# A fused block of three attentions, a feed-forward, experts and a mixture of depths: one output product and two batches of comparisons put in another order

## The chip, the cores and the metric

The kernel runs on one core of a Trainium2 chip. The metric is the device time of one execution in microseconds (us). The engines of a core run their own instruction queues: TensorE (PE) multiplies matrices and transposes, VectorE (DVE) reduces, adds and splits numbers, ScalarE (ACT) does exponents, Gelus and copies, GpSimd (POOL) does normalizations, powers and indirect transfers, and SyncE (SP) issues DMAs. They meet through semaphores: an instruction that waits holds up everything behind it in its queue.

## The reference

Eight batches of 256 tokens with 256 features go through four residual steps. Only the last two touch the change.

```
x = x + attention_block(layernorm(x), ctx)      # cross, self, feed-forward
x = x + experts(layernorm(x))                   # top 2 of 8, capacity
x = x + mha(layernorm(x), ctx, ctx)             # 16 heads: here "third attention"
x = x + mod(layernorm(x))

def mod(h):                                     # mixture of depths
    scores = einsum('bsd,d->bs', h, w_router)
    top_scores, top_idx = top_k(scores, 128)    # half the tokens of a batch
    selected = take(h, top_idx)
    processed = gelu(selected @ W1 + b1) @ W2 + b2
    return h.at[top_idx].add(sigmoid(top_scores) * processed)
```

## The kernel before

An attention works in items: item n is one batch of one attention, and items 16 to 23 are batches 0 to 7 of the third one. For an item TensorE makes scores for eight pairs of heads twice: once for the row maxima that VectorE reduces (L785), once transposed for ScalarE's Exp (L807, into T_PS). Behind two Exps each a group of probability products (L853) fills half of a bank, ScalarE copies it to oext (L1164), and behind the fourth such copy TensorE transposes oext (L827). VectorE divides by the sums, TensorE transposes back (L249), ScalarE and VectorE write aT_hi and aT_lo, the upper and lower half of each number, and TensorE makes the output product with three matmuls for each tile (mm3, L216 to L218: high times high, low times high, high times low). VectorE adds its result to xres (L1645, semaphore res_s). The transposes of the next item's oext wait for that res_s.

The mixture of depths works in pairs of batches: pair j is batches 2j and 2j+1. mod_select(j) turns scores into a one-hot selection. GpSimd spreads a batch's scores, TensorE transposes them (L982), and VectorE counts for each token how many scores stand above it (L1818 and L1819, twice each), adds (trank, L1820), and compares with the slot numbers (oh, L1824). I call these eight instructions a batch's comparisons. TensorE then gathers with that one-hot (L996), transposes it (L1001), and mod(j) does the first product (mm3 with hT and m_lo), ScalarE's Gelus (L1258) and copies (L1268), VectorE's lower halves (L1841), the second product for each batch (mm3 with kst and qst), VectorE's result in three instructions (L1850 to L1852: proc, its upper and lower half), TensorE's scatter product with the transposed one-hot (L1055 and L1056), and VectorE's addition to xres (L1859, x4 for a pair).

No scheduler decides the order on an engine. Every part is a generator that yields the time at which its next step is due, and side_by_side runs the step with the least due time, on each engine apart. The tables PE_ORDER, ACT_ORDER, POOL_ORDER and DVE_ORDER override this: an entry "A": "B" puts step A straight behind step B, and behind(...) chains a list of them. "attention 22.23" is step 23 of item 22 on that engine. On TensorE the steps of an item from 9 on are: Exp scores 9, 10, 11, products 12, scores 13, 14, products 15, scores 16, 17, 18, products 19 and 20, the transposes of oext 21, those of the divided output 22, the output product 23. "mod 0.0" to "mod 0.3" are four quarters of the first half of pair 0's first product, six matmuls each. On VectorE "mod_select j.1" is the comparisons of the second batch of pair j, and "mod j.5" the result of that pair's second batch.

On ScalarE the four Gelus of pair 0's first half wait for the last of these four quarters, and the order there is: copy of item 23's third product group, first Gelu, copy of the fourth group, the other Gelus. The first Gelu needs a table load of its own.

Of the kernel before, what the change touches and what calls it, by code (L numbers as in the profile page):

```python
# [94 lines left out]
def behind(*steps):  # L95

    return dict(zip(steps[1:], steps))


def build(nc, x, ctxT, mask, wA, colA, rowA, fi, fo, fib, rw, rb, ein, eout, wC, colC, rowC, colV, w1, w2, b1, out):  # L100
# [21 lines left out]
    with scope[0] as root:  # L122
# [312 lines left out]
        def mod_bank(i):  # L435
# [24 lines left out]
            **behind("mod_select 0.2", "attention 23.14", "attention 23.15", "mod_select 1.0", "attention 22.22", "attention 23.16", "mod 0.0", "mod 0.1", "attention 23.17",  # L460
                     "mod 0.2", "mod 0.3", "attention 23.18", "attention 23.19", "attention 23.20", "attention 22.23", "attention 23.21", "mod 0.4", "mod 0.5",
                     "attention 23.22", "mod 0.6", "mod 0.7", "attention 23.23", "mod_select 1.1", "mod_select 1.2", "mod 0.8", "mod_select 2.0"),
        }
        ACT_ORDER = {
# [33 lines left out]
            **behind("mod_select 0.1", "attention 21.10", "attention 21.11", "attention 20.13", "attention 21.12", "attention 22.8", "mod_select 0.2", "attention 22.9",  # L498
                     "mod_select 1.0", "mod_select 1.1", "attention 21.13", "attention 22.10", "attention 23.8", "attention 22.11", "attention 22.12", "mod 0.0", "mod 0.1",
                     "attention 23.9", "attention 23.10", "mod 0.2", "mod 0.3", "mod_select 1.2", "attention 23.11", "attention 23.12"),  # L500
        }

        with nc.Block() as block:
# [1411 lines left out]
```

How the kernel before makes its waits and increments, by code:

```python
    def __call__(self, ins):  # L64
        self.n += 1
        ins.then_inc(self.sem, 1)
        self.eng.wait_ge(self.sem, self.n)
# [439 lines left out]
                def setup():  # L507
# [16 lines left out]
                    sp.dma_start(rows[:, 2:8, :], rowA[2:8].unsqueeze(0).to_broadcast([P, 6, D])).then_inc(sm["small_ld"], 16)  # L524
                    sp.dma_start(fibc[:], fib).then_inc(sm["small_ld"], 16)
                    sp.dma_start(rbr[:], rb.to_broadcast([P, 8])).then_inc(sm["small_ld"], 16)
                    sp.dma_start(rw_raw[:], rw.rearrange("(k p) n -> p k n", p=P)).then_inc(sm["small_ld"], 16)
                    sp.dma_start(b1c[:], b1).then_inc(sm["small_ld"], 16)
                    sp.wait_ge(sm["ident_s"], 3)
                    for i in range(NE * CAP // P):
                        yield 28 + 4 * i
                        sp.dma_start(moe_in[i * P:(i + 1) * P, :], zeros[:]).then_inc(sm["zero_out"], 16)
                    sp.dma_start(moe_out[NE * CAP:NE * CAP + 1, :], zeros[0:1, :]).then_inc(sm["zero_out"], 16)
                    yield STEP * B + 32
                    sp.wait_ge(sm["h_ready"], B)
                    sp.dma_start(rows[:, R_CO:R_CBE + 1, :], rowA[R_FO:R_FBE + 1].unsqueeze(0).to_broadcast([P, 3, D])).then_inc(sm["rowsF_ld"], 16)
                    yield T_F0 + 8
                    sp.wait_ge(sm["h_ready"], NA)
# [537 lines left out]
                def mask_rows():  # L1076
                    yield -93
                    act.wait_ge(sm["mask_s"], 1)
                    for c in range(2):
```

## Time and profile before

| | |
|---|---|
| median of 3 runs | 857.49 us (852.05 to 859.93) |
| the profiled execution's own time | 855.1 us |
| its span | 853.1 us |
| TensorE busy, share of the span | 729.4 us, 85% |
| VectorE | 648.7 us, 76% |
| ScalarE | 455.6 us, 53% |
| GpSimd | 409.2 us, 48% |
| mean granted TensorE clock | 0.929 |

The span runs from the first to the last instruction on the core; the execution's own time has some 2 us around it. A row of a timeline gives the start, the duration, engine, line, operation, output and inputs, and in brackets how long the engine had been idle and what released it. Neighbouring equal instructions are merged into one row. A matmul's duration covers its whole way through the array, so matmuls in a group start closer together than they last.

### The profile page before, as it was taken

Reading aid. Unit: us, or ns where it says so; the run is one execution under the profiler, and the core shown is the slowest. Engines: PE = TensorE matmul, PEld = TensorE weight load, DVE = VectorE, ACT = ScalarE, POOL = GpSimd, SP = SyncE. Lnnn points to the kernel's source line nnn. Section 1 sums busy time; section 2 is a strip of 40 time slices with the busy share of each in tenths; the row PEclk is TensorE's granted clock in tenths of the full one; section 3 lists DMA queues with packets and bytes.
Section 4 is the critical chain, followed back from the end, with each engine's and each line's share of the span. In section 5 each row is a group of like instructions: output and inputs, shape, how many; then the busy total and the mean of one; then the engine's idle time right before and its main releaser. Section 6 shows DMA issues by size and latency. Waiting matters only on the chain.

```text
span 853.1 us, 18296 instructions
## 1 busy us (share of the span) xinstructions
PE 729.4 (85%) x7218; PEld 607.8 (71%) x7218; DVE 648.7 (76%) x1250; ACT 455.6 (53%) x695; POOL 409.2 (48%) x395
## 2 busy tenths in 40 slices
PE   5788999999999778999894599993677889888897
PEld 4666777777777546999883599992455657656897
DVE  7768888888888653799887377756876889877864
ACT  4256777777777566656432144421145557667342
POOL 7874654534665454624466241107577236473400
PEclk9979999999999899999995699996769989999999
DMA  6687786679776602000030577634586637500011
GB/s 190 131 136 119 140 125 99 104 118 140 115 107 102 88 3 99 26 1 22 24 128 11 154 235 245 194 68 110 86 148 95 98 60 106 85 2 2 13 39 49
DMA packets 57065, 81.47 MB, mean 95 GB/s; under 512 B 8434, under 2 KB 35057, under 8 KB 56932
## 3 DMA queue, kind: packets, MB, share of 16 engines
q1 hardware_dynamic: 53730, 74.11, 45.1%
q0 software_dynamic: 3072, 6.04, 2.9%
q8 instruction: 57, 0.93, 0.5%
q10 hardware_dynamic: 178, 0.16, 0.1%
q14 instruction: 28, 0.23, 0.1%
HBM read 36.74 MB, written 10.11 MB: 55 GB/s over the span
## 4 chain that ended last, share of the span: by engine, by line
PE 61%; DVE 19%; issue 7%; DMA 4%; ACT 4%; POOL 2%; SPq 1%; another core or an unknown queue 0%; ACTq 0%; DVEq 0%; POOLq 0%
PE ps L216 13%; PE ps L218 11%; PE ps L217 11%; PE ps L785 7%; PE ps L853 7%; DVE nmax L1623 6%; PE ps L807 5%; ACT prob L1151 2%; PE ps L827 2%; DMA kst<-k_parts 2%; POOL gat L1469 1%; PE ps L240 1%; PE ps L249 1%; SPq L568 1%; DMA gat<-moe_out,slu 1%
## 5 line engine op out<-in xcount | busy, mean ns | idle before, releaser
L1623 DVE TENSOR_REDUCE nmax<-ps 128x4 f32<-128x1024 f32 x192 | 234.3, 1223 | 69.8 <-PE ps L785 65.0
L1151 ACT ACTIVATE prob<-ps 128x1024 f32<-128x1024 f32 x192 | 196.4, 1023 | 70.4 <-PE ps L807 64.5
L1380 POOL TENSOR_TENSOR rstd<-var,half 128x2 f32<-128x2 f32 x56 | 43.9, 785 | 243.7 <-DVE var L1550 173.0
L785 PE MATMUL ps<-kst,qst 50*128 50x256 f32 (+1 forms) x768 | 99.6, 339 | 34.0 <-DVE nmax L1623 27.3
L853 PE MATMUL ps<-prob,vext 128*32 128x256 f32 x1536 | 107.0, 398 | 1.2 <-ACT oext L1164 1.2
L785 PEld LDWEIGHTS ps<-kst,qst 50*128 50x128 f32 (+1 forms) x768 | 60.9, 196 | 66.0 <-DVE nmax L1623 44.8
L807 PE MATMUL ps<-qst,kst 51*128 51x256 f32 (+1 forms) x768 | 83.3, 296 | 14.6 <-ACT prob L1151 13.8
L807 PEld LDWEIGHTS ps<-qst,kst 51*128 51x128 f32 (+1 forms) x768 | 61.6, 194 | 21.4 <-ACT prob L1151 17.1
L853 PEld LDWEIGHTS ps<-prob,vext 128*32 128x32 f32 x1536 | 41.2, 112 | 33.2 <-issue 4.1
L1164 ACT ACTIVATE oext<-ps 128x256 f32<-128x256 f32 x96 | 36.9, 385 | 31.7 <-PE ps L827 17.4
L1388 POOL TENSOR_SCALAR hres<-xres,mv,rstd 128x256 f32<-128x256 f32 x42 | 52.1, 1246 | 2.2
L1469 POOL DMA_INDIRECT gat<-moe_out,slu x32 | 33.4, 1043 | 37.4 <-DMA moe_out<-vext 28.7
L216 PE MATMUL ps<-hT_hi,w_hi 128*128 128x256 f32 x160 | 49.7, 311 | 1.8 <-DVE hT_lo L1553 1.8
L218 PE MATMUL ps<-hT_lo,w_hi 128*128 128x256 f32 x160 | 45.8, 286 | 0.0
L1457 POOL DMA_INDIRECT moe_in<-hres,slu x32 | 32.8, 1024 | 25.1 <-DVE slu L1759 17.1
L240 PE MATMUL ps<-ident,hres 128*128 128x128 f32 x108 | 20.3, 319 | 26.9 <-DVE hres L1600 19.6
L1388 POOL TENSOR_SCALAR res<-res,mv,rstd 128x256 f32<-128x256 f32 x32 | 39.0, 1226 | 1.7
L217 PE MATMUL ps<-hT_hi,w_lo 128*128 128x256 f32 x128 | 36.9, 288 | 0.0
L1098 ACT ACTIVATE k_parts<-ps,cols 128x256 fp32r<-128x256 f32 x48 | 20.1, 472 | 31.2 <-PE ps L218 28.3
L216 PEld LDWEIGHTS ps<-hT_hi,w_hi 128*128 128x128 f32 x160 | 31.2, 195 | 6.9 <-DVE hT_lo L1553 2.7
L1182 ACT ACTIVATE prob<-ps,fibc 128x256 f32<-128x256 f32 x64 | 27.3, 471 | 16.3 <-PE ps L218 15.9
L216 PE MATMUL ps<-w_hi,qst 128*128 128x256 f32 x128 | 35.9, 281 | 0.0
(287 smaller groups left out, 2315.3 us busy)
## 6 DMA issues: line engine op xcount, KB each, us to landing
kst<-k_parts SPq DMA_DIRECT2D x138, 128.0 KB, 5.1
qst<-q_parts SPq DMA_DIRECT2D x132, 128.0 KB, 3.8
e_raw<-in_ein SPq DMA_DIRECT2D x7, 1024.0 KB, 5.2
e_raw<-in_eout SPq DMA_DIRECT2D x7, 1024.0 KB, 6.1
ctx_raw<-in_ctxT SPq DMA_DIRECT2D x16, 256.0 KB, 5.5
out<-xres SPq DMA_DIRECT2D x8, 256.0 KB, 2.2
moe_in<-zeros SPq DMA_DIRECT2D x14, 128.0 KB
moe_out<-vext SPq DMA_DIRECT2D x7, 256.0 KB, 5.9
```

Of the source, the lines that this page charges most:

```text
L216: pe.matmul(dst, lhs[0], rhs[0], start=first, stop=False)
L217: pe.matmul(dst, lhs[1], rhs[0], start=False, stop=False)
L218: return pe.matmul(dst, lhs[0], rhs[1], start=False, stop=last)
L785: last = pe.matmul(score_pair(n, p)[:, 512 * s + S * t:512 * s + S * (t + 1)], qst[j][a:b, p, t * P:(t + 1) * P], kst[j][a:b, p, :], start ...
L807: last = pe.matmul(T_PS[:, 512 * s + S * t:512 * s + S * (t + 1)], kst[j][a:b, p, t * P:(t + 1) * P], qst[j][a:b, p, :], start=True, stop= ...
L853: last = pe.matmul(half_bank[32 * i:32 * i + 32, :], vext[n % VSET][:, t, s * HG + p, :], probs[p % 4][:, s, t, :], start=(t == 0), stop=( ...
L1151: act.activation(probs[p % 4][:].rearrange("p i t s -> p (i t s)"), T_PS, ACT.Exp).then_inc(sm["exp_done"], 1)
L1164: act.activation(oext[:, u, :], PV_PS[:, S * (u % 2):S * (u % 2 + 1)], ACT.Copy).then_inc(sm["o_ev"], 1)
L1380: last = gp.tensor_tensor(rstd[i][:], var[i][:], half[:], ALU.pow)
L1388: last = gp.tensor_scalar(dst[:, t, :], src[:, t, :], mv[i][:, t, 0:1], rstd[i][:, t:t + 1], ALU.subtract, ALU.mult)
L1469: gp.indirect_dma_start(gat[:, b % 4, t, r, :], None, moe_out, bass.IndirectOffsetOnAxis(ap=slu[:, TB * b + t, r:r + 1], axis=0), bounds_c ...
L1623: dve.tensor_reduce(nmax[n % 2][:, :, :, p].rearrange("p t s -> p s t"), score_pair(n, p).rearrange("p (s t k) -> p s t k", s=2, t=TB), AX ...
```

## The change

Three entries of the order tables change; no instruction, wait or buffer is added or removed on any engine, and ScalarE, GpSimd and SyncE keep their order.

```diff
@@ PE_ORDER @@
             **behind("mod_select 0.2", "attention 23.14", "attention 23.15", "mod_select 1.0", "attention 22.22", "attention 23.16", "mod 0.0", "mod 0.1", "attention 23.17",
-                     "mod 0.2", "mod 0.3", "attention 23.18", "attention 23.19", "attention 23.20", "attention 22.23", "attention 23.21", "mod 0.4", "mod 0.5",
+                     "attention 22.23", "attention 23.18", "attention 23.19", "mod 0.2", "mod 0.3", "attention 23.20", "attention 23.21", "mod 0.4", "mod 0.5",
@@ DVE_ORDER @@
+            "mod_select 2.1": "mod 0.5", "mod_select 3.1": "mod 1.5",
```

The new line moves all line numbers behind it up by one: L807 of before is L808 of the change.

TensorE before, from item 23's scores for its seventh Exp to the transposes of its oext. The matmuls on hT_hi and hT_lo are pair 0's first product, those on w_hi, w_lo and aT item 22's output product; of each twelve the first three stand:

```order
L807 MATMUL ps<-qst,kst 128x256 x4
L216 MATMUL ps<-hT_hi,w_hi 128x256
L217 MATMUL ps<-hT_hi,m_lo 128x256
L218 MATMUL ps<-hT_lo,w_hi 128x256
...
L807 MATMUL ps<-qst,kst 128x256 x4
L853 MATMUL ps<-prob,vext 32x256 x16
L216 MATMUL ps<-w_hi,aT_hi 128x256
L217 MATMUL ps<-w_hi,aT_lo 128x256
L218 MATMUL ps<-w_lo,aT_hi 128x256
...
L827 MATMUL ps<-ident,oext 128x64 x16
```

The same place in the change:

```order
L808 MATMUL ps<-qst,kst 128x256 x4
L216 MATMUL ps<-w_hi,aT_hi 128x256
L217 MATMUL ps<-w_hi,aT_lo 128x256
L218 MATMUL ps<-w_lo,aT_hi 128x256
...
L808 MATMUL ps<-qst,kst 128x256 x4
L854 MATMUL ps<-prob,vext 32x256 x8
L216 MATMUL ps<-hT_hi,w_hi 128x256
L217 MATMUL ps<-hT_hi,m_lo 128x256
L218 MATMUL ps<-hT_lo,w_hi 128x256
...
L854 MATMUL ps<-prob,vext 32x256 x8
L828 MATMUL ps<-ident,oext 128x64 x16
```

Item 22's output product went up, in front of the last scores, and the twelve of pair 0 went down between the two last probability groups.

VectorE before, from the end of batch 4's comparisons (trank, oh) over batch 5's to the result of batch 1 (proc and its halves in qst):

```order
L1820 TENSOR_TENSOR trank<-above 128x2
L1824 TENSOR_SCALAR oh<-wraw,trank 128x128 x2
L1818 TENSOR_SCALAR cmp,above<-ps,score 128x256
L1819 SCALAR_TENSOR_TENSOR cmp,above<-ps,score,wraw 128x256
L1818 TENSOR_SCALAR cmp,above<-ps,score 128x256
L1819 SCALAR_TENSOR_TENSOR cmp,above<-ps,score,wraw 128x256
L1820 TENSOR_TENSOR trank<-above 128x2
L1824 TENSOR_SCALAR oh<-wraw,trank 128x128 x2
L1850 TENSOR_TENSOR proc<-ps,rows 128x256
L1851 CAST qst<-proc 128x256
L1852 TENSOR_TENSOR qst<-proc,qst 128x256
```

The same place in the change:

```order
L1821 TENSOR_TENSOR trank<-above 128x2
L1825 TENSOR_SCALAR oh<-wraw,trank 128x128 x2
L1851 TENSOR_TENSOR proc<-ps,rows 128x256
L1852 CAST qst<-proc 128x256
L1853 TENSOR_TENSOR qst<-proc,qst 128x256
L1819 TENSOR_SCALAR cmp,above<-ps,score 128x256
L1820 SCALAR_TENSOR_TENSOR cmp,above<-ps,score,wraw 128x256
L1819 TENSOR_SCALAR cmp,above<-ps,score 128x256
L1820 SCALAR_TENSOR_TENSOR cmp,above<-ps,score,wraw 128x256
L1821 TENSOR_TENSOR trank<-above 128x2
L1825 TENSOR_SCALAR oh<-wraw,trank 128x128 x2
```

Batch 1's result stands now in front of batch 5's comparisons, not behind them. The same exchange is made one pair later, with batch 3's result and batch 7's comparisons.

## Rows read from the trace of the kernel before

**Rows 1.** The page, part 4: the chain that ended last, by engine.

```profile
PE 61%; DVE 19%; issue 7%; DMA 4%; ACT 4%; POOL 2%; SPq 1%; another core or an unknown queue 0%; ACTq 0%; DVEq 0%; POOLq 0%
```

**Rows 2.** Windows of 10 us: engines' busy time, clock, DMA share, GB/s.

```profile
740.00:750.00 10.00, 7.50 (x74) 5.90 (x78) 6.32 (x11) 4.85 (x7) 9.84 (x9) 0.83 0.41 54
...
800.00:810.00 10.00, 8.06 (x68) 7.86 (x68) 9.72 (x36) 2.72 (x6) 3.41 (x4) 1.00 0.04 13
```

**Rows 3.** Timeline of TensorE, item 23's last products and what follows.

```profile
779.50 0.50 PE L807 MATMUL ps<-qst,kst 49*128 49x256 f32 x4
...
781.54 0.50 PE L807 MATMUL ps<-qst,kst 49*128 49x256 f32 x4
781.97 1.07 PE L853 MATMUL ps<-prob,vext 128*32 128x256 f32 x16
783.64 1.07 PE L853 MATMUL ps<-prob,vext 128*32 128x256 f32 x16 [0.59 <-ACT oext L1164]
...
787.16 0.71 PE L827 MATMUL ps<-ident,oext 64*128 64x64 f32 x16 [0.88 <-DVE xres L1645]
...
791.96 0.39 PE L216 MATMUL ps<-w_hi,aT_hi 128*128 128x256 f32 x1 [0.48 <-DVE aT_lo L1556]
```

**Rows 4.** Timeline of ScalarE, the first Gelu between the last copies.

```profile
783.11 0.38 ACT L1164 ACTIVATE oext<-ps 128x256 f32<-128x256 f32 x1
783.51 1.28 ACT L1258 ACT_TABLE_LOAD   x1
784.80 0.48 ACT L1258 ACTIVATE mg<-ps,b1c 128x256 f32<-128x256 f32 x1
785.18 0.38 ACT L1164 ACTIVATE oext<-ps 128x256 f32<-128x256 f32 x1
```

**Rows 5.** Timeline of ScalarE, another table load, in the routing.

```profile
439.50 1.28 ACT L1197 ACT_TABLE_LOAD   x1
441.85 0.23 ACT L1197 ACTIVATE rt<-rt 128x32 f32<-128x32 f32 x1 [1.07 <-DVE rt L1731]
```

**Rows 6.** Timeline of VectorE around item 22's and item 23's output.

```profile
778.41 0.69 DVE L1556 TENSOR_TENSOR aT_lo<-ps,aT_hi 128x512 fp32r<-128x512 f32 x1 [2.15 <-ACT aT_hi L1157]
...
786.32 0.69 DVE L1645 TENSOR_TENSOR xres<-ps,xres 128x512 f32<-128x512 f32 x1 [1.63 <-PE ps L218]
787.91 0.37 DVE L1629 RECIPROCAL rsum<-ps 128x16 f32<-128x16 f32 x2 [0.90 <-PE ps L827]
...
791.22 0.68 DVE L1556 TENSOR_TENSOR aT_lo<-ps,aT_hi 128x512 fp32r<-128x512 f32 x1
```

**Rows 7.** Timeline of VectorE, comparisons and results of the pairs.

```profile
803.55 0.48 DVE L1818 TENSOR_SCALAR_CACHE_REDUCE cmp<-ps,score 128x256 f32<-128x256 f32 x1
...
806.00 0.42 DVE L1850 TENSOR_TENSOR proc<-ps,rows 128x256 f32<-128x256 f32 x1
...
806.78 0.43 DVE L1852 TENSOR_TENSOR qst<-proc,qst 128x256 fp32r<-128x256 f32 x1
...
809.39 1.28 DVE L1841 TENSOR_TENSOR kst<-mg,qst 128x512 fp32r<-128x512 f32 x2
...
819.54 0.48 DVE L1818 TENSOR_SCALAR_CACHE_REDUCE cmp<-ps,score 128x256 f32<-128x256 f32 x1
```

**Rows 8.** Timeline of TensorE, the scatter products and what stands around them.

```profile
805.05 0.28 PE L218 MATMUL ps<-hT_lo,w_lo 128*128 128x256 f32 x1
807.26 0.39 PE L1055 MATMUL ps<-qst 128*128 128x256 f32 x1 [1.94 <-DVE qst L1852]
...
812.80 0.36 PE L216 MATMUL ps<-kst,qst 128*128 128x256 f32 x1
...
822.87 0.28 PE L218 MATMUL ps<-hT_lo,w_lo 128*128 128x256 f32 x1
823.25 0.38 PE L1055 MATMUL ps<-qst 128*128 128x256 f32 x1
```

**Rows 9.** Lines L1820 and L1824 from 750 us: least, median, greatest duration in ns.

```profile
L1820 DVE TENSOR_TENSOR trank<-above x8: 160/160/1215, 765.5 to 821.4; 128x2 f32<-128x2 f32 x8
L1824 DVE TENSOR_SCALAR oh<-wraw,trank x16: 279/286/1304, 766.6 to 821.8; 128x128 f32<-128x128 f32 x16
```

## The prediction

> **What bounds the kernel now.** I read the chain that ended last first: TensorE holds 61% of it, VectorE 19% and bare issue 7% [rows 1]. So a microsecond counts where TensorE stands still, or where VectorE stands in the chain between two TensorE groups. The orders of all engines are equal up to 779.50 us, so only the last 73.6 us can move. I then read the granted clock in windows of 10 us: 1.00 (2.4 GHz) at 800 to 810, but 0.83 at 740 to 750, where TensorE was busy for only 7.50 us [rows 2]. Where work moves, the array is at its upper level. Last I read the timelines of TensorE, ScalarE and VectorE around both edits, looking only for the waits in brackets. TensorE waits there 0.59 us in front of item 23's last probability product, 0.88 us in front of the transposes of its output, 0.48 us in front of item 23's own output product [rows 3], and later 1.94 us in front of the scatter product of batch 1 [rows 8].
>
> **Edit 1, TensorE: item 22's output product goes up, half of pair 0's first product goes down.** Nothing is added or removed; two groups of 12 matmuls of equal shape (128*128 by 128x256) change places. Before, twelve stood between the scores at 779.50 and those at 781.54. The probability products at 781.97 show that a score group takes 0.43, so twelve take 2.04 - 0.43 = 1.61 us [rows 3]. Now the twelve of item 22 stand there, and the scores at 781.54 stay where they are. The condition is that item 22's lower half aT_lo is there by 779.93: it was written from 778.41 for 0.69, by 779.10 [rows 6], a margin of 0.83 us.
>
> Next come the probability products of rows 781.97, one group of about 1.00. The 12 matmuls that went down follow at 782.97 and fill what was the 0.59 wait; they end at 784.58. The last probability group then starts at 784.58 instead of 783.64 and ends, with the 1.07 of its row, at 785.65 [rows 3]. That is 0.94 later, so what follows matters. Before, three things stood behind it: the output product (1.61), VectorE's addition to xres (786.32, 0.69), and a wait of 0.88; the transposes started at 787.16 [rows 3, 6]. Now the product is long done. VectorE's own queue reaches the addition at 786.32 - 1.63 = 784.69, the start of its idle time, and ends it at 785.38 [rows 6]. What the transposes wait for is then ScalarE's copy of the last probability product. On the row before, a product that ended at 783.04 was copied from 783.11 to 783.49, and TensorE went on at 783.64 [rows 3, 4]: 0.07 + 0.38 + 0.15 = 0.60. So the transposes start at 785.65 + 0.60 = 786.25 instead of 787.16, a gain of **0.91 us**.
>
> On ScalarE that copy stands behind the first Gelu of pair 0, and this Gelu now needs the half that went down, ready at 784.58 instead of 781.54. Before, it started at 784.80, because a table load ran from 783.51 to 784.79 [rows 4]. The load hides the 3.04 us only if it doesn't stand behind the Gelu's wait itself. The routing's load shows that it doesn't: it ran at 439.50 for 1.28, and only then its Exp waited 1.07 us for VectorE, to 441.85 [rows 5]. So this move costs nothing; were the cover gone, it would cost 784.58 + 1.28 - 784.80 = 1.06 on the Gelu.
>
> Behind the transposes TensorE and VectorE run as before, relative to them: VectorE does the division of item 23, the statistics of item 22, two lower halves of pair 0 and aT_lo without a gap of weight, from 787.91 until 791.22 + 0.68, and TensorE takes item 23's output product at 791.96, 4.80 us behind the start of the transposes [rows 3, 6]. The 0.48 wait there stays, since VectorE's queue makes it. I take 0.9 for edit 1, and not the 0.91 + 0.48 = 1.39 that the idle times alone would give.
>
> **Edit 2, VectorE: the comparisons of batches 5 and 7 behind the results of batches 1 and 3.** Again nothing is added. I give the times of the trace before; both engines come here 0.9 earlier by edit 1, which cancels. Before, VectorE compared batch 5 from 803.55 and came to batch 1's result (three instructions) at 806.00, so the comparisons take 2.45; the result ended 806.78 + 0.43 = 807.21 and TensorE went on at 807.26 [rows 7, 8]. Now the result starts at 803.55 and ends at 804.76. TensorE's last matmul in front started at 805.05, and the step inside such groups is 0.12 (twelve in 1.61, with the first slower), so it can go on at 805.17 [rows 8]. It does, with 0.4 us to spare, and gains 807.26 - 805.17 = **2.09 us**.
>
> What is late next: the comparisons themselves, by the 1.21 of the result. They end at 807.21, as the result did before, so VectorE's queue behind is unmoved: its lower halves of pair 1 start at 809.39 and the first is ready about 0.65 later, 810.04. TensorE wants that one for the product that started at 812.80 and now would at 810.71 [rows 7, 8]. The one-hot of batch 5, wanted in front of that product at 810.67 - 2.09 by the same count, is there with over 1 us. All else behind (Gelus, their lower halves, the last normalization) is released by TensorE or comes in the same queue, so it shifts along.
>
> In pair 3 the same swap meets nearly no wait: the last matmul in front started at 822.87 and the next at 823.25, where 822.99 was possible, so **0.26 us**. Here VectorE has nothing to spare: it starts the comparisons of batch 7 at 819.54 [rows 7] and now would wait until TensorE's product is out, some tenths, in a queue that has slack behind it. I count nothing for that.
>
> **Sum.** 0.9 + 2.1 + 0.26 = 3.26, so about 3.2 us less from the profiled execution's 855.1 us (span 853.1), 851.9 us. That execution lies 2.4 under the median of the runs shown, 857.49; the same 3.2 off the median gives **854.3 us**, 0.4% less.
>
> **Rivals.** (a) *The Gelu's load is not hidden.* If it stands behind the wait, the Gelu starts at 785.86, ends 0.38 later (785.18 - 784.80 in rows 4), the copy takes 0.38 more, and with 0.15 the transposes start at 786.77: edit 1 gives 0.39, the sum 2.7, the time 854.8. Rows 5 speak against it. The Trainium skill (ScalarE: Activation LUTs, "What ACT_TABLE_LOAD costs") gives a switch of sets as the load plus a drain, about 2.66 us together. By that page the Gelu would begin 2.66 behind 784.58, the transposes 1.0 later than before, and edits 1 and 2 together would give 1.4, an estimate. This trace disagrees on the drain: the Gelu started 0.01 behind its load [rows 4].
>
> (b) *Edit 2 pays only in part, since VectorE is slower than I count.* The small operation trank takes 0.16 at the median but 1.22 once in this stretch, and the mask oh 0.28 but up to 1.30 [rows 9]. One such stretch more (about 1.0) in front of batch 1's result passes the margin of 0.4 and eats 0.6; two of them eat 1.6. Then the sum is 1.6 to 2.6, the time 854.9 to 855.9. The Trainium skill (GPSIMD Engine Reference, "Specifications") says that GpSimd's SBUF interface is shared with VectorE, with contention for instructions with two SBUF inputs. trank is of that kind, so the trace agrees; the result's last instruction is too. Against it: GpSimd's work of that stretch follows VectorE's statistics and shifts with them.
>
> (c) *Slower: item 22's product waits in front of the last scores.* It now stands in the chain of scores and exponents. If aT_lo comes later than 779.93, every us of that is a us in front of the scores at 781.54, the exponent and all behind. From 0.83 us of lateness on it costs, and from 0.83 + 3.26 = 4.1 us on the kernel is slower than before; at 5 us it is 858.4. aT_lo hangs on ScalarE and a VectorE that idled before it [rows 6], and its order in both queues is unchanged, so I see nothing that would make it late.
>
> (d) *The chip doesn't show it:* other idle of TensorE near the end takes the gain back, time 857.5. The order behind has no fixed clock to meet, only the final stores, which follow the results.
>
> (e) *The clock falls in the last stretch.* At 740 to 750 the granted clock was 0.83 with TensorE busy for 7.50 [rows 2]. Such a window costs 10 x 0.17 = 1.7 us, and three of them turn the result to slower, 859.4 at most. The change takes idle time away, so it speaks for a high clock rather than against.
>
> **How the numbers follow.** Both edits pay as counted, 851.0 to 854.8 around the forecast: 0.66. (a) 0.06, (b) 0.14, (c) 0.03, (d) 0.07, (e) 0.04. The likeliest case is 854.3. The largest gain that the waits allow is 0.59 + 0.88 + 0.48 + 2.09 + 0.26 = 4.3, so 853.2 of the median; the runs shown reach 852.05 to 859.93, more than the change moves, and a median of new runs can lie a few us off. With (b) and (d) inside, the range is 850.8 to 858.2. A measurement of this kernel can tell about 1%, 8.6 us, from no change. No case reaches a gain of that size, and (c) or (e) would have to be multiplied to lose as much: faster 0.02, same 0.96, slower 0.02.
>
> **What would show it.** In the changed kernel's profile: twelve matmuls on w_hi,aT_hi in front of the last scores with no wait on aT_lo; no wait between the two last probability groups; the transposes of oext released by ScalarE's oext and not by VectorE's xres; the Gelu at once behind its table load; and the wait of 1.94 on the scatter product gone. I'm wrong if ScalarE idles between the table load and the Gelu, if TensorE's transposes start later than 5.6 us behind the last scores (787.16 - 781.54), if the 1.94 comes back in front of the next product as a wait on kst, or if the span shortens by less than 1.6 or more than 4.3.

## The result and the profile after

The changed kernel took 853.09 us (median of 20 runs, 846.07 to 858.33), the kernel before in the same comparison 857.07 us (20 runs, 851.63 to 861.86). The two medians differ by 4.0 us. The ratio that the comparison gives for all these runs is 0.9944, with a 95% interval of 0.9921 to 0.9967: 4.8 us less, 2.8 to 6.8. Forecast were 854.3 us and 3.2 us less.

The profiled execution of the change has a span of 853.9 us, 0.8 more than that of before. That is no contradiction. Up to the seventh of item 23's eight Exp scores (779.50 us before) the orders are equal, and behind them both kernels do twelve matmuls of the same shape, so the last scores stand 2.04 us behind the seventh in both. These last scores came at 781.54 us before [rows 3] and at 785.82 in this execution. From there to the end of the span it was 853.1 - 781.54 = 71.6 us before and is 853.9 - 785.82 = 68.1 us now, 3.5 less. So the traces are compared from these last scores on.

TensorE's timeline of the change, from item 22's output product to item 23's (start, duration, then the instructions, and in brackets idle time and releaser):

```profile
784.22 0.39 PE L216 MATMUL ps<-w_hi,aT_hi 128*128 128x256 f32 x1
784.44 0.28 PE L217 MATMUL ps<-w_hi,aT_lo 128*128 128x256 f32 x1
...
785.82 0.51 PE L808 MATMUL ps<-qst,kst 49*128 49x256 f32 x4
786.26 1.07 PE L854 MATMUL ps<-prob,vext 128*32 128x256 f32 x16
788.88 1.07 PE L854 MATMUL ps<-prob,vext 128*32 128x256 f32 x16
790.45 0.71 PE L828 MATMUL ps<-ident,oext 64*128 64x64 f32 x16 [0.51 <-ACT oext L1165]
...
795.26 0.38 PE L216 MATMUL ps<-w_hi,aT_hi 128*128 128x256 f32 x1 [0.48 <-DVE aT_lo L1557]
```

Item 22's product starts without a wait on aT_lo. The wait of 0.59 between the probability groups [rows 3] is gone, filled by pair 0's twelve matmuls. The transposes start 4.63 us behind the last scores, not 5.62, and ScalarE's copy releases them, not VectorE's xres. The 0.48 on aT_lo stays.

ScalarE's timeline of the change, where the copy and the first Gelu meet:

```profile
787.80 1.28 ACT L1259 ACT_TABLE_LOAD   x1
789.09 0.47 ACT L1259 ACTIVATE mg<-ps,b1c 128x256 f32<-128x256 f32 x1
790.02 0.38 ACT L1165 ACTIVATE oext<-ps 128x256 f32<-128x256 f32 x1 [0.45 <-PE ps L854]
```

The load ran while TensorE still computed what the Gelu waits for, and the Gelu began 0.01 behind it, as in [rows 4]. The copy waited for TensorE, not for the Gelu.

VectorE's timeline of the change, item 22's addition and item 23's division, then batch 1's result and, further on, batch 3's:

```profile
788.89 0.69 DVE L1646 TENSOR_TENSOR xres<-ps,xres 128x512 f32<-128x512 f32 x1
791.21 0.37 DVE L1630 RECIPROCAL rsum<-ps 128x16 f32<-128x16 f32 x2 [1.63 <-PE ps L828]
...
806.81 0.42 DVE L1851 TENSOR_TENSOR proc<-ps,rows 128x256 f32<-128x256 f32 x1
...
807.59 0.42 DVE L1853 TENSOR_TENSOR qst<-proc,qst 128x256 fp32r<-128x256 f32 x1
...
820.99 0.42 DVE L1851 TENSOR_TENSOR proc<-ps,rows 128x256 f32<-128x256 f32 x1 [0.26 <-PE ps L218]
```

And TensorE's timeline where the 1.94 us of [rows 8] stood:

```profile
808.37 0.28 PE L218 MATMUL ps<-hT_lo,w_lo 128*128 128x256 f32 x1
808.48 0.28 PE L1056 MATMUL ps<-qst 128*128 128x256 f32 x1
```

Batch 1's result is ready at 808.01, and its scatter product follows the matmul in front in the ordinary step of 0.11, with nothing between.

### The profile page after: what moved, and what is told of

It is laid out like the page before. It is cut to its first block, busy times and chain, and to the rows that moved or that the text cites. A ratio compares the mean times of both kernels' runs of the same rounds, so it can differ in the third digit from the quotient of the medians.

```text
span 853.9 us, 18296 instructions
## 1 busy us (share of the span) xinstructions
PE 733.5 (86%) x7218; PEld 611.5 (72%) x7218; DVE 647.7 (76%) x1250; ACT 455.5 (53%) x695; POOL 409.1 (48%) x395
## 4 chain that ended last, share of the span: by engine, by line
PE 61%; DVE 16%; issue 6%; DMA 6%; POOL 4%; ACT 3%; SPq 3%; POOLq 0%; DVEq 0%; ACTq 0%
PE ps L216 13%; PE ps L217 11%; PE ps L218 11%; PE ps L854 7%; PE ps L786 7%; DVE nmax L1624 5%; PE ps L808 5%; DMA kst<-k_parts 2%; SPq L569 2%; ACT prob L1152 2%; PE ps L828 2%; POOL gat L1470 1%; PE ps L249 1%; PE ps L240 1%; DMA gat<-moe_out,slu 1%
## 5 line engine op out<-in xcount | busy, mean ns | idle before, releaser
L786 PEld LDWEIGHTS ps<-kst,qst 50*128 50x128 f32 (+1 forms) x768 | 61.4, 197 | 67.6 <-DVE nmax L1624 44.7
L808 PE MATMUL ps<-qst,kst 51*128 51x256 f32 (+1 forms) x768 | 83.6, 296 | 12.7 <-ACT prob L1152 11.9
L808 PEld LDWEIGHTS ps<-qst,kst 51*128 51x128 f32 (+1 forms) x768 | 61.7, 194 | 19.4 <-ACT prob L1152 14.7
```

The source lines that it names most:

```text
L786: last = pe.matmul(score_pair(n, p)[:, 512 * s + S * t:512 * s + S * (t + 1)], qst[j][a:b, p, t * P:(t + 1) * P], kst[j][a:b, p, :], start ...
L808: last = pe.matmul(T_PS[:, 512 * s + S * t:512 * s + S * (t + 1)], kst[j][a:b, p, t * P:(t + 1) * P], qst[j][a:b, p, :], start=True, stop= ...
```

## The experiments

Twelve more executions were profiled: nine other orders or kernels, the kernel before twice more and the change once more. All times below count from the start of item 23's last scores (L807 or L808) in the same profile. I use three marks behind it: the start of the transposes of item 23's oext, the first matmul of batch 6's scatter product, and the end of the span. The second mark is the better one for the whole, since the last store's way to memory differs from profile to profile (more on that in the last section).

| kernel | wait in front of batch 1's scatter | transposes | batch 6's scatter | end | lower clock behind that wait |
|---|---|---|---|---|---|
| before | 1.94 | 5.62 | 65.91 | 71.6 | no |
| before, second | 1.94 | 5.60 | 65.90 | 71.6 | no |
| before, third | 1.93 | 5.62 | 67.42 | 73.1 | yes |
| edit 1 alone | 1.93 | 4.63 | 66.46 | 72.2 | yes |
| pair 3's half alone | 1.94 | 5.62 | 67.02 | 72.7 | yes |
| wait longer | 2.62 | 5.61 | 69.33 | 75.0 | yes |
| wait filled | 0.52 | 5.62 | 65.90 | 71.6 | no |
| pair 2's half alone | none | 5.62 | 63.73 | 69.4 | no |
| edit 2 alone | none | 5.62 | 63.31 | 70.1 | no |
| the change | none | 4.63 | 62.37 | 68.1 | no |
| the change again | none | 4.63 | 62.34 | 68.0 | no |
| product earlier | none | 4.63 | 62.37 | 68.0 | no |
| statistics first | none | 4.63 | 61.68 | 69.2 | no |
| load behind the copy | none | 4.63 | 63.00 | 70.7 | no |

**Each edit alone, and the change again.** Edit 1 alone:

```diff
-                     "mod 0.2", "mod 0.3", "attention 23.18", "attention 23.19", "attention 23.20", "attention 22.23", "attention 23.21", ...
+                     "attention 22.23", "attention 23.18", "attention 23.19", "mod 0.2", "mod 0.3", "attention 23.20", "attention 23.21", ...
```

> The change's first edit alone: item 22's output product in front of item 23's last scores, pair 0's twelve matmuls behind them, VectorE as before. Theory A (both edits act where they stand and add up): from the start of item 23's last scores to the transposes of its oext 4.6 us instead of 5.6, the wait for VectorE's xres gone, a wait of 0.5 for ScalarE's copy in its place; from the last scores to the end of the span 70.6 us (before 71.6, the change 68.1); the 1.94 us in front of the scatter product still there. Time about 0.1% under before, ratio 0.999. Theory B (the change's timed gain of 0.6% is more than these waits, something else of edit 1 gives it): 69.5 us or less from the last scores on, ratio 0.997 or lower.

Edit 2 alone:

```diff
+            "mod_select 2.1": "mod 0.5", "mod_select 3.1": "mod 1.5",
```

> The change's second edit alone: on VectorE the results of batches 1 and 3 in front of the comparisons of batches 5 and 7, TensorE as before. Theory A: the transposes stay 5.6 us behind the last scores, the 1.94 us wait in front of the scatter product goes, and from the last scores to the end of the span it takes 69.1 us (before 71.6). Ratio about 0.997. Theory B (only both edits together give the gain, since each alone only moves a wait): 71 us or more, ratio 1.000.

The change itself once more:

> The change itself once more, on the chip of the three runs beside it. Theory A: 68.1 us from the last scores to the end of the span again, ratio 0.996 as the waits give; the first measurement's 0.9944 then lay on the low side of its interval by what the 780 us ahead scatter. Theory B: ratio 0.994 again, with a shorter way to the last scores than before's.

Measured, on one chip with 35 runs of the kernel before (median 859.7 us): edit 1 alone 858.83 us, ratio 1.0004 (0.9981 to 1.0027). Edit 2 alone 856.35 us, ratio 0.9971 (0.9944 to 0.9998). The change 854.09 us, ratio 0.9952 (0.9927 to 0.9977), 4.1 us less (the medians differ by 5.6). That ratio lies between the 0.996 and the 0.994 of its two theories and decides for neither.

In the profiles the transposes move by 0.99 with edit 1 and by nothing with edit 2, as theory A has it. The change again is 62.34 to batch 6's scatter and 68.0 to the end, as the first time. Edit 2 alone is 63.31 to batch 6's scatter, 2.60 less than before; its end, 70.1, is a us later than A's 69.1 by the last store. But the way to the end of edit 1 alone is 72.2 us, neither A's 70.6 nor B's 69.5. It is longer than before, though its waits are the same and the transposes come earlier. TensorE's timeline of edit 1 alone shows why:

```profile
809.35 0.39 PE L1055 MATMUL ps<-qst 128*128 128x256 f32 x1 [1.93 <-DVE qst L1852]
809.57 0.28 PE L1056 MATMUL ps<-qst 128*128 128x256 f32 x1
...
810.17 0.28 PE L218 MATMUL ps<-hT_lo,w_hi 128*128 128x256 f32 x1
810.29 0.28 PE L216 MATMUL ps<-hT_hi,w_lo 128*128 128x256 f32 x1
810.40 0.35 PE L217 MATMUL ps<-hT_hi,m_lo 128*128 128x256 f32 x1
810.55 0.42 PE L218 MATMUL ps<-hT_lo,w_lo 128*128 128x256 f32 x1
810.77 0.42 PE L216 MATMUL ps<-hT_hi,w_hi 128*128 128x256 f32 x1
...
813.76 0.34 PE L218 MATMUL ps<-hT_lo,w_hi 128*128 128x256 f32 x1
813.93 0.28 PE L216 MATMUL ps<-hT_hi,w_lo 128*128 128x256 f32 x1
814.05 0.28 PE L217 MATMUL ps<-hT_hi,m_lo 128*128 128x256 f32 x1
```

About 1.1 us behind the restart the step between matmuls goes from 0.12 to 0.21, and back at 813.9. The granted clock in windows of 5 us from the scatter product's start, edit 1 alone (columns: stretch, busy time of TensorE, its weight loads, VectorE, ScalarE and GpSimd, then clock, DMA share, GB/s):

```profile
809.35:814.35 5.00, 5.00 (x29) 5.00 (x30) 3.40 (x10) 0.86 (x2) 0.40 (x1) 0.66 0.32 105
814.35:819.35 5.00, 5.00 (x45) 5.00 (x45) 2.47 (x7) 3.79 (x9) 0.00 (x0) 1.00 0.00 0
```

and the same two windows of the kernel before, in the profile from which I forecast:

```profile
807.26:812.26 5.00, 5.00 (x43) 5.00 (x44) 3.41 (x10) 2.25 (x7) 0.40 (x1) 1.00 0.31 105
812.26:817.26 5.00, 4.61 (x40) 4.37 (x39) 3.93 (x12) 2.39 (x5) 0.40 (x1) 1.00 0.01 3
```

TensorE is busy 5.00 of 5.00 us in both and does 29 matmuls in the one and 43 in the other. At the mark of batch 6, edit 1 alone stands at 66.46, while before less 0.99 would be 64.92: the lower clock cost 1.54 us. This opened a question that the forecast had not asked: does this fall belong to edit 1, or to the wait of 1.9 us?

**The halves of edit 2.** Only pair 2's line, and only pair 3's:

```diff
+            "mod_select 2.1": "mod 0.5",
```

> Of the second edit only the first half: batch 1's result in front of batch 5's comparisons. Theory A: 69.4 us from the last scores to the end of the span (before 71.6), since this half gives 2.1 and no wait comes in its place; in front of the next scatter product the start of TensorE stays 0.26 late. Theory B (VectorE's comparisons, now 1.2 us later, hold up the next products): 70.5 us or more, with a wait of TensorE on kst or oh.

```diff
+            "mod_select 3.1": "mod 1.5",
```

> Of the second edit only the other half: batch 3's result in front of batch 7's comparisons. Theory A: it gives the 0.26 us that TensorE's matmuls show as a gap, 71.3 us from the last scores to the end (before 71.6), and VectorE idles some 0.3 us in front of the result. Theory B (it costs, since VectorE waits for TensorE there with seven comparisons behind it): 71.6 us or more.

Pair 2's half: 69.4 us to the end as expected, and at batch 6's scatter 63.73 instead of 65.91, so 2.18. No wait on kst or oh took its place. Pair 3's half gave somewhat more than the 0.26 that was expected of it, and something else hid it. Its end came at 72.7 us, where B had 71.6 or more, but the cause is the clock again: windows from its scatter product's start,

```profile
810.22:815.22 5.00, 5.00 (x29) 5.00 (x30) 3.41 (x10) 0.86 (x2) 0.40 (x1) 0.66 0.31 105
815.22:820.22 5.00, 5.00 (x45) 5.00 (x44) 2.49 (x7) 3.79 (x9) 0.00 (x0) 1.00 0.00 0
```

Against the execution of before that has the same fall (before, third: 67.42), its 67.02 is 0.40 less. Against pair 2's half (63.73), both halves together (63.31) are 0.42 less. So pair 3's half is worth 0.4. VectorE idles 0.25 us in front of batch 3's result there, as A said; that costs nothing.

**The kernel before twice more.** No edit.

> The kernel before once more, for its profile. In two of three profiles with the 1.94 us wait in front of the scatter product (both of the single-edit kernels that keep it) the granted clock fell to 1.2 GHz right behind that wait for some 3.4 us and cost about 1.6 us; in the profile of before it did not. Theory A (the fall hangs on the wait and comes by chance): it falls in some executions of before too; then 73.2 us from the last scores to the end of the span, else 71.6. Theory B (the fall comes from what those two kernels changed): never here, 71.6.

> The kernel before a third time, for the same reason. Theory A: 73.2 us from the last scores to the end if the clock falls behind the 1.94 us wait, 71.6 if not; at least one of these two repeats shows the fall. Theory B: 71.6 in both.

The second shows 71.6 us and the clock at 1.00 behind the wait. The third shows 73.1 us; its wait and the window from the restart on:

```profile
812.39 0.39 PE L1055 MATMUL ps<-qst 128*128 128x256 f32 x1 [1.93 <-DVE qst L1852]
```

```profile
812.39:817.39 5.00, 5.00 (x29) 5.00 (x30) 3.40 (x10) 0.86 (x2) 0.40 (x1) 0.66 0.31 105
```

Theory A holds: the unchanged kernel has the fall too, in one of its three profiles, so the fall is not owed to either edit. At batch 6's scatter it stands at 67.42 instead of 65.91, a price of 1.51 us. Over all five profiles that keep the 1.93 or 1.94 us wait, the clock fell in three.

**The wait filled, and the wait made longer.** Filled: twelve matmuls repeat the last quarter of pair 1's first half.

```diff
-                        for m in range(4 * half, 4 * half + 4):
+                        for m in [*range(4 * half, 4 * half + 4)] + [3, 3] * (j == 1 and half == 0):
```

> The kernel before, with twelve matmuls more in front of the 1.94 us wait: the last quarter of pair 1's first half is computed three times instead of once into the same place, which changes no result. They fill 1.41 us of the wait, so about 0.5 us of it is left, and TensorE's next product starts where it did. Theory A (the wait also costs clock): no fall behind it, 71.6 us from the last scores to the end in every profile, and a ratio to before of 0.999, more work in no more time. Theory B (idle time there is all that it costs): ratio 1.000; more matmuls raise the chance of nothing.

Longer: batch 1's result behind item 22's score as well.

```diff
+            "mod 0.5": "attention 22.13",
```

> The kernel before, with batch 1's result behind item 22's score too, so that TensorE waits longer in front of the scatter product: 2.7 us instead of 1.9. Theory A (a longer wait makes the fall of the clock behind it likelier): the clock falls in the profile, 72.3 us plus about 1.6, so 73.9, from the last scores to the end, ratio 1.002 to 1.003. Theory B (only the added idle counts): 72.3 us and the clock at 1.00 throughout, ratio 1.001.

The filled kernel does twelve matmuls more and comes to batch 6's scatter at 65.90, where before is at 65.91. Its wait is 0.52, and the clock behind it stays up:

```profile
815.20 0.39 PE L1055 MATMUL ps<-qst 128*128 128x256 f32 x1 [0.52 <-DVE qst L1852]
```

```profile
815.20:820.20 5.00, 5.00 (x43) 5.00 (x44) 3.40 (x10) 3.63 (x10) 0.40 (x1) 1.00 0.31 105
```

The longer kernel waits 2.62 us and starts at the lower clock at once; the first matmul of the scatter product takes 0.58:

```profile
812.95 0.58 PE L1056 MATMUL ps<-qst 128*128 128x256 f32 x1 [2.62 <-DVE qst L1853]
```

```profile
812.95:817.95 5.00, 5.00 (x23) 5.00 (x24) 2.80 (x6) 0.16 (x1) 0.00 (x0) 0.50 0.31 105
817.95:822.95 5.00, 5.00 (x41) 5.00 (x40) 1.31 (x3) 3.64 (x9) 0.00 (x0) 0.89 0.00 0
```

Pair 3's half, with a wait of 1.94, had the lower clock at the restart too. There it lasted for 3.4 us from the restart, here for some 6 (0.50 in the first window and 0.89 in the second).

The longer kernel comes to batch 6's scatter at 69.33, 3.42 later than before. Of this 0.70 is the longer wait (its scatter product starts at 26.42 and not 25.72), and 2.7 is clock. Its end at 75.0 us is later than A's 73.9, since the fall lasted longer than in the other kernels. The timed runs, on one chip with 23 of the kernel before: 859.18 us filled, ratio 1.0000 (0.9968 to 1.0033), and 861.02 us longer, ratio 1.0012 (0.9977 to 1.0048). Neither interval separates the theories, because the effects are near 1 us. The profiles do: with the wait of 1.9 us or more the clock fell behind it in four of six, and with the wait gone or filled in none of eight. How often it falls with the wait of 1.9 us rests on five profiles and is known only roughly; "wait filled" and "wait longer" have one profile each.

**The product one group earlier still.**

```diff
-                     ... "attention 23.16", "mod 0.0", "mod 0.1", "attention 23.17", "attention 22.23", "attention 23.18", ...
+                     ... "attention 23.16", "attention 22.23", "attention 23.17", "mod 0.0", "mod 0.1", "attention 23.18", ...
```

> The change, with item 22's output product one score group earlier still, in front of item 23's seventh scores, and pair 0's first twelve matmuls behind them. aT_lo is ready about 1.2 us after TensorE comes to it there. Theory A (every us of waiting in that chain is a us): a wait of about 1.2 us on aT_lo, and from item 23's sixth scores to the end 73.4 us (the change 72.1, before 75.6). Theory B (the exponents, on which TensorE waits anyway in this stretch, hide it): the wait is there, but the end comes at 72.1 to 72.5.

TensorE's timeline, item 23's sixth scores, item 22's product, the seventh scores:

```profile
773.96 0.48 PE L808 MATMUL ps<-qst,kst 49*128 49x256 f32 x4
775.63 0.38 PE L216 MATMUL ps<-w_hi,aT_hi 128*128 128x256 f32 x1 [1.20 <-DVE aT_lo L1557]
...
777.24 0.50 PE L808 MATMUL ps<-qst,kst 49*128 49x256 f32 x4
```

The wait is 1.20 us, and from the sixth scores to the end it takes 847.3 - 773.96 = 73.3 us, against 853.9 - 781.76 = 72.1 in the change. Every us of that wait is a us. This was the forecast's slower rival (c), made to happen: its price was right (at batch 6's scatter, counted from the sixth scores, this kernel is 1.26 behind the change). In the change itself TensorE comes to the product at 784.22, and aT_lo was written by 783.38 (from 782.69 for 0.69), so the margin held. This kernel's one time, 850.33 us, is nevertheless among the lowest here: its last scores came at 779.28, because of what lies ahead of the change.

**The load without its cover.**

```diff
-                     ... "attention 23.11", "mod 0.0", "attention 23.12", "mod 0.1", ...
+                     ... "attention 23.11", "attention 23.12", "mod 0.0", "mod 0.1", ...
```

> The change, with ScalarE's copy of the fourth probability product in front of the first Gelu, so that the table load stands behind that copy and is covered by nothing. Theory A (a load costs 1.28 us and hides wherever ScalarE would idle): transposes 4.6 us behind the last scores as in the change, first Gelu about 1.3 us behind the copy, item 23's output product waits 1.2 us on aT_lo instead of 0.48, and from the last scores to the end 68.8 us instead of 68.1. Theory B (a load costs 2.66 us, with a drain): first Gelu 2.7 us behind the copy, 70.2 us to the end.

ScalarE's timeline:

```profile
786.20 0.38 ACT L1165 ACTIVATE oext<-ps 128x256 f32<-128x256 f32 x1 [2.23 <-PE ps L854]
786.61 1.28 ACT L1259 ACT_TABLE_LOAD   x1
787.90 1.57 ACT L1259 ACTIVATE mg<-ps,b1c 128x256 f32<-128x256 f32 x4
```

The Gelu follows 1.32 us behind the copy's end, not 2.7: theory A. The transposes stay at 4.63, item 23's output product waits 1.15 us on aT_lo instead of 0.48, and batch 6's scatter comes at 63.00 instead of 62.37, 0.63 later. The end, 70.7, is later than A's 68.8 by the last store.

**A step further.** On VectorE item 22's statistics in front of item 23's division, into the 1.63 us in which VectorE idles in the change.

```diff
-                     ... "attention 22.10", "attention 23.8", "attention 22.11", "attention 22.12", "mod 0.0", ...
+                     ... "attention 22.10", "attention 22.11", "attention 22.12", "attention 23.8", "mod 0.0", ...
```

> The change, and besides on VectorE item 22's statistics (1.1 us) in front of item 23's division instead of behind it, into the 1.6 us in which VectorE idles there. Theory A (VectorE's queue makes the 0.48 us wait of item 23's output product): that wait goes, the product starts 9.0 us behind the last scores instead of 9.4, and from the last scores to the end it takes 67.6 us instead of 68.1; ratio to before about 0.996. Theory B (the wait hangs on ScalarE's aT_hi, which comes behind the Gelus' copies): wait and 68.1 us unchanged.

VectorE's timeline of that kernel:

```profile
788.66 0.75 DVE L1543 BATCH_NORM_STATS2 bn<-xres 128x6 f32<-128x256 f32 x2
789.44 0.25 DVE L1549 BATCH_NORM_AGGREGATE mv<-bn 128x2 f32<-128x6 f32 x2
789.73 0.17 DVE L1551 TENSOR_SCALAR var<-mv 128x2 f32<-128x2 f32 x1
790.25 0.37 DVE L1630 RECIPROCAL rsum<-ps 128x16 f32<-128x16 f32 x2 [0.36 <-PE ps L828]
...
792.88 0.69 DVE L1557 TENSOR_TENSOR aT_lo<-ps,aT_hi 128x512 fp32r<-128x512 f32 x1 [0.36 <-ACT aT_hi L1158]
```

The statistics fit into the gap, aT_lo now waits for ScalarE, and TensorE's output product has no wait left; batch 6's scatter comes at 61.68, 0.69 less than in the change. Theory A, with a somewhat larger gain than the 0.48. Its end, 69.2 and not A's 67.6, is late by the last store. Timed, 854.33 us, ratio 0.9952 (0.9921 to 0.9983), the same as the change beside it (854.09). On its mechanism this is the best version of all, but the timed runs can't tell it from the change.

## Why the prediction was right, and where its terms were off

**Edit 1.** Forecast 0.9, measured 0.99 at the transposes and 0.96 at batch 0's scatter product (19.36 instead of 20.32 behind the last scores). The step from ScalarE's copy to TensorE was taken as 0.15 from one pair of rows; here the copy ends at 790.40 and TensorE starts at 790.45, 0.05. The condition (aT_lo there in time) held: no wait in front of the twelve matmuls. The remaining 0.48 was VectorE's queue, as said; the kernel with the statistics first shows it.

**The table load.** Covered, as argued from the routing's load. The Trainium skill (ScalarE: Activation LUTs, "What ACT_TABLE_LOAD costs") adds a drain to the load, some 2.66 us together. Both the change (0.01 us from load to Gelu) and the kernel with the uncovered load (1.32 us from copy to Gelu) disagree with that for this place. Rival (a) is out.

**Edit 2.** Forecast 2.09 and 0.26, measured 2.09 at the start of batch 1's scatter product and 2.18 with what follows, and 0.4 for pair 3. In both cases the forecast left out one thing: the first matmul behind the wait takes a longer step to the next (0.22 from 809.35 to 809.57 in edit 1 alone, 0.12 in a running group). In the change the scatter product follows the group in front without a break, and its first step is 0.12 too. The longer step is not owed to idle time alone: item 22's product has it straight behind the scores, with no wait (784.22 to 784.44). The margins behind held: no wait on kst or oh was added, and the one on GpSimd's spread is 0.39 as before. The stretched trank of 1.22 us appeared again (once, in front of batch 1's result) and was inside the count, so rival (b) did not come. The change's timelines of VectorE and GpSimd show what it goes with:

```profile
805.16 1.22 DVE L1821 TENSOR_TENSOR trank<-above 128x2 f32<-128x2 f32 x1
805.07 1.29 POOL L1428 TENSOR_TENSOR xres<-xres,hres 128x512 f32<-128x512 f32 x1
```

It ended at 806.38, 0.02 behind GpSimd's addition (805.07 + 1.29 = 806.36). Before, it ended at 803.12 and that addition at 803.10. So the stretch is tied to one GpSimd addition, and it would come again wherever the two meet; no experiment here moved them apart.

**The sum.** 0.96 + 2.18 + 0.4 = 3.54, measured 65.91 - 62.37 = 3.54; forecast 3.26. So the waits are accounted for within 0.3 us. The 854.3 us came out 1.2 too high; 0.4 of that is the kernel before, which came at 857.07 and not at the 857.49 that I had started from.

**A sign that was badly chosen.** I had written that I'm wrong if the span shortens by less than 1.6. It grew by 0.8. The sign compared whole spans of two executions, whose last scores lie 4.3 us apart for reasons ahead of the change; from the last scores on the span is 3.5 shorter. All the other signs, which stand on waits and releasers, held.

**What the sum lacked.** The timed gains are 4.8 us (2.8 to 6.8) and 4.1 us (2.0 to 6.3 by the interval of 0.9927 to 0.9977). Both intervals hold 3.5, so the timed runs alone ask for nothing more; the profiles do. I had read the clock as 1.00 in the tail and had weighed it only as rival (e), a danger to the changed kernel. In the runs it is a cost of the kernel before: its 1.94 us wait brings the lower clock in part of its executions, at 1.5 us each time. With the three of five that the profiles show, that is 0.9 us more on average, and 3.5 + 0.9 = 4.4; with the one of three of the unchanged kernel it is 0.5, and the sum 4.0. The size of this term is an estimate from so few profiles, and no timed comparison shows it: edit 2 alone, which takes the wait away, gave 2.5 us (0.2 to 4.8), and the filled wait 0.0. That the term exists is shown. That it goes with this wait is shown by four falls in six profiles (the longer wait with them) against none in eight. Edit 1 alone measured 1.0004; its 0.99 lies inside that interval, and the clock term can't be the reason, since edit 1 and the kernel before both have the wait.

Rivals (c) and (d) didn't come; (c) was produced on purpose and costs us for us.

## What to carry to other kernels

Price an edit in a static order from the next wait behind it, not from the idle time it fills: filling 0.59 delayed one group by 0.96 (it started 3.06 and not 2.10 us behind the last scores), and what counted was which releaser came last at the transposes. Then look at what the idle time does to TensorE's clock: one profile at full clock doesn't show that a wait of 1 or 2 us is free of that cost, so take several profiles of the kernel before. And compare profiles from the last common point: the 780 us ahead of this change moved that point between 779.28 and 789.46 us, three times what the change was worth.

## What the hardware showed that I had not expected

A single idle time of TensorE of 1.93 to 1.94 us, after a group of matmuls that ran closely, was followed by the lower clock (1.2 GHz, steps of 0.21 us instead of 0.12) in three of five profiles of that wait. It began between 0 and 1.2 us behind the restart and cost 1.5 us each time. After 2.62 us of idle the clock was low at the restart and the fall cost 2.7 us. After 0.52 us, in one profile, and where the place had no wait at all, in seven, it did not come. The twelve useless matmuls in the gap cost nothing: batch 6's scatter came at 65.90 with them and at 65.91 without.

Nor does it take 1.9 us. In the 24 us ahead of the last scores TensorE waits three times for 1.08 to 1.12 us, on VectorE's maxima or ScalarE's exponents. In five of the fourteen profiles the granted clock fell there too, for 3.4 us, each time within 1.6 us of the restart from such a wait. In the filled kernel, for example, scores at 775.15 us had waited 1.11 us, and the clock was down from 776.7. From that restart to the last scores it then took 14.31 us, against 12.77 in the profiles where the clock stayed up, so that fall cost 1.5 us. In the other nine profiles the same waits left the clock at 1.00. So a wait of 1.1 us is followed by the fall as well, in some executions and not in others, and such falls are part of what moves the last scores from one execution to the next. What decides it in one execution these traces don't show.

The last store varies as well. The view of the transfers gives a median of 2.2 us from issue to landing for the stores of the last stretch in the change,

```profile
out<-xres SPq DMA_DIRECT2D x3, 256.0 KB, 2.2
```

and 3.4 us in the kernel with the statistics first:

```profile
out<-xres SPq DMA_DIRECT2D x2, 256.0 KB, 3.4
```

That moves the end of the span by one to two us: from batch 6's scatter to the end it is 5.7 us in the change and 7.6 in that kernel. It was as late in two more of the fourteen profiles, edit 2 alone (3.1 us) and the load behind the copy (3.5). I found nothing in the order that explains it, and leave its cause open.
